# Cross-attention normalised in channel layout, with the denominators summed by VectorE

## Chip, cores and metric

One core of one Trainium2 chip. The metric is the device time of one launch in microseconds, and lower is better. The kernel before takes 371.97 us, the median of 3 runs (371.9 to 372.0).

## What is computed

A decoder layer over 16 sequences of 128 tokens with 256 channels: a retention block (8 heads of 32), a causal cross-attention with 16 heads of 16 channels, and a feed-forward block (256 to 1024 to 256, its own weights for each pair of sequences), each behind a layer norm and with a residual. The change touches only the cross-attention:

```python
scores = jnp.einsum('bhqd,bhkd->bhqk', qh, kh) * scale
scores = jnp.where(causal, -jnp.inf, scores)
attn = jax.nn.softmax(scores, axis=-1)
out = jnp.einsum('bhqk,bhkd->bhqd', attn, vh)
out = out.transpose(0, 2, 1, 3).reshape(b, s, DIM)
return out @ Wo + bo
```

## The kernel before

The work is cut into 8 steps of two sequences (NB = 2, T = 256 tokens). Three blocks run as a software pipeline: body(i) does retention of step a = i, cross-attention of step b = i - 1 and the feed-forward block of step c = i - 2. Bodies 0, 1 and 2 are written out, bodies 3 to 6 are a loop, and bodies 7 (no further retention input), 8 (no retention) and 9 (feed-forward only) are written out again. Each engine has its own body with a fixed order of instructions, and semaphores tie the engines together. All eight PSUM banks are in use and named: a0, a1, b0, b1k, b2k, b3, c0, c1; the trace leaves digits out, so it calls them a, b, b1k, b2k and c.

Attention of one step goes in eight units u, four per sequence (PR = 4), with four heads each (G = 4). For a unit, TensorE writes the scores; VectorE takes the maxima (negmax, L912); ScalarE takes the exponentials (prob, L596, four instructions); TensorE transposes the four 128x128 tiles into bank b1k (L1344); ScalarE copies the even units to probT (L558), VectorE the odd ones (L919); TensorE multiplies by v_pad, 32 columns a head: 16 values, a one, and zeros (`with_values`, L1347). So the sum of the probabilities comes out of the same matmul as channel 16 of each head. prob and probT have four buffers.

After four units (a sequence), ScalarE copies the products to pvT (`pv_out`, L639), TensorE turns them back into token layout with four transposes (`values_to_tokens`, L1366, instruction line L1371), VectorE takes the reciprocal of the sums (rden, L928) and multiplies (att, L930). After both sequences, TensorE transposes att again, into channel layout (`attention_transposes`, instruction line L1223), ScalarE copies it to attT_hi (L558), VectorE writes the remainder to attT_lo (L862), and TensorE multiplies by xWo (`attention_out`, L1379).

Around the change, in the order of each queue in a body of the loop:

- VectorE, from the last hidden split (L905) on: probT(1), varA (L1045, L1047), statistics of the next x (L842 to L849), maxima 4, probT(3), maxima 5, retT (L1109), maxima 6 and 7, xnA (L857), outT (L1127, two), probT(5), x (L1137, the retention's output with its residual), divide(0), probT(7), statistics of it, divide(1), cTB_lo (L862), xnB (L857), attT_lo (L862), x2b (L962), x (L956, the attention's output).
- TensorE, from the transposes of unit 5 on: a piece of the feed-forward product, values_to_tokens(0), the product of outT with W_sb, transposes of unit 6, values of units 4 and 5, transposes of xnA, transposes of unit 7, feed-forward, values of units 6 and 7, transposes of the context c_in, gate piece 0, values_to_tokens(1), gate pieces 1 and 2, attention_transposes, keys (cTB, xWk), attention_out.
- GpSimd takes the reciprocal square roots (rsA, rsB, rsC, rstA; L453), the low parts of the feed-forward weights (w_lo, L460 and L466), and sums with biases (L473, L480).

## Time and profile before

| | |
|---|---|
| median of 3 runs | 371.97 us |
| the profiled execution, whole | 369.38 us |
| its span, first to last instruction | 367.6 us |
| granted TensorE clock | 1.000 of full speed |
| TensorE matmul busy | 338.3 us, 92% |
| VectorE busy | 254.6 us, 69% |
| ScalarE busy | 238.9 us, 65% |
| GpSimd busy | 163.5 us, 44% |

Busy time says how long an engine had something in it, not whether it set the pace: matmuls overlap in the array, so a busy TensorE can still have been fed late. In a timeline, a row gives the start in us from the span's start, the busy time of the row, engine and line, what is written and read, and in brackets the idle time of the engine before the row with what ended it. Consecutive VectorE instructions overlap a little: of two 128x512 operations the second starts about 0.60 us after the first, though each is listed with 0.68 or 0.69 us.

### The profile page before, as it was taken

What the parts mean: (1) busy time and instruction counts of PE and PEld (TensorE: products, weight loads), DVE (VectorE), ACT (ScalarE), POOL (GpSimd) and SP (SyncE); (2) the same over time, 40 slices, a digit from 0 to 9 for tenths busy, and PEclk for the clock granted to TensorE, in tenths of its full rate; (3) what the DMA queues carried; (4) which work ended last, traced back from release to release, by engine and by line L of the source; (5) the groups of instructions that cost most, each with busy time, mean ns of one, the idle gap of its engine ahead of it and who ended that gap; (6) DMA issues with size and microseconds to landing.
All of it is one profiled execution on the core that took longest, in us unless ns stands there. A gap on an engine that the chain in (4) does not pass through costs nothing.

```text
span 367.6 us, 8998 instructions
## 1 busy us (share of the span) xinstructions
PE 338.3 (92%) x3283; PEld 280.1 (76%) x3299; DVE 254.6 (69%) x555; ACT 238.9 (65%) x586; POOL 163.5 (44%) x148
## 2 busy tenths in 40 slices
PE   7878679999999999999999999999999998989697
PEld 3657457987789877987789867987789866858596
DVE  5674786677766976677775976678765966482974
ACT  4552663776756866677847766677848764787551
POOL 4237150364615366363625457362634550445340
PEclk9999999999999999999999999999999999999999
DMA  5940102022031400413023400404014300013300
GB/s 151 307 172 1 31 2 107 37 62 85 1 112 78 144 0 17 171 33 110 0 66 120 143 0 14 169 7 137 0 47 141 116 6 10 30 16 116 116 29 30
DMA packets 22314, 26.97 MB, mean 73 GB/s; under 512 B 2896, under 2 KB 20112, under 8 KB 22288
## 3 DMA queue, kind: packets, MB, share of 16 engines
q1 hardware_dynamic: 21472, 26.52, 22.3%
q8 instruction: 17, 0.28, 0.3%
q10 hardware_dynamic: 816, 0.10, 0.2%
q14 instruction: 9, 0.07, 0.1%
HBM read 24.51 MB, written 2.10 MB: 72 GB/s over the span
## 4 chain that ended last, share of the span: by engine, by line
PE 77%; DVE 9%; issue 7%; ACT 4%; POOL 1%; DMA 1%; ACTq 0%; DVEq 0%; POOLq 0%
PE c L1208 22%; PE a L1208 16%; PE b L1208 14%; PE b1k L1344 7%; PE b1k L1208 6%; PE b2k L1208 4%; DVE negmax L912 2%; PE c L1371 2%; ACT prob L596 1%; ACT probT L558 1%; PE a L1223 1%; DVE scD L893 1%; PE b2k L1223 1%; DMA wk_c<-in_L_attn_Wk 1%; PE a L1301 1%
## 5 line engine op out<-in xcount | busy, mean ns | idle before, releaser
L460 POOL TENSOR_TENSOR w_lo<-w_in,w_hi 128x512 fp32r<-128x512 f32 x32 | 40.8, 1305 | 30.4 <-ACT w_hi L558 26.3
L596 ACT ACTIVATE prob<-b,negmax 128x128 f32<-128x128 f32 x124 | 36.1, 398 | 25.4 <-DVE negmax L912 25.4
L1344 PE MATMUL b1k<-ident,prob 128*128 128x128 f32 x256 | 40.0, 279 | 9.3 <-ACT probT L558 4.5
L466 POOL TENSOR_TENSOR w_lo<-w_in,w_hi 128x512 fp32r<-128x512 f32 x28 | 35.5, 1287 | 28.6 <-ACT w_hi L558 26.8
L453 POOL TENSOR_TENSOR rstA<-varA,minus_half 128x16 f32<-128x16 f32 x8 | 23.4, 2927 | 49.2 <-DVE varA L1047 49.2
L1344 PEld LDWEIGHTS b1k<-ident,prob 128*128 128x128 f32 x256 | 28.1, 140 | 17.3 <-ACT prob L596 7.2
L558 ACT ACTIVATE w_hi<-w_in 128x512 fp32r<-128x512 f32 x64 | 39.1, 653 | 2.6 <-PE b L1208 2.6
L1208 PE MATMUL c<-xTC_hi,w_hi 128*128 128x256 f32 x108 | 31.8, 294 | 0.8 <-DVE xTC_lo L862 0.8
L919 DVE COPY probT<-b1k 128x512 f32<-128x512 f32 x32 | 22.0, 687 | 13.1 <-PE b1k L1344 13.0
L1208 PE MATMUL c<-w_hi,h_hi 128*128 128x256 f32 x96 | 30.8, 321 | 0.1
L1208 PE MATMUL c<-xTC_lo,w_hi 128*128 128x256 f32 x108 | 30.5, 282 | 0.0
L1208 PE MATMUL c<-xTC_hi,w_lo 128*128 128x256 f32 x108 | 30.5, 282 | 0.0
L573 ACT ACTIVATE h_in<-c,b_cur 128x256 f32<-128x256 f32 x54 | 22.6, 472 | 11.4 <-PE c L1208 11.2
L912 DVE TENSOR_REDUCE negmax<-b 128x4 f32<-128x512 f32 x31 | 21.3, 687 | 12.5 <-PE b2k L1208 8.7
L1208 PE MATMUL c<-w_hi,h_lo 128*128 128x256 f32 x96 | 27.0, 281 | 0.0
L1208 PE MATMUL c<-w_lo,h_hi 128*128 128x256 f32 x96 | 26.9, 280 | 0.0
L453 POOL TENSOR_TENSOR rsC<-mvC,minus_half 128x2 f32<-128x2 f32 x8 | 5.7, 710 | 45.2 <-DVE mvC L849 45.2
L905 DVE TENSOR_TENSOR h_lo<-h_in,h_hi 128x512 fp32r<-128x512 f32 x32 | 24.5, 767 | 1.1
L558 ACT ACTIVATE probT<-b1k 128x512 f32<-128x512 f32 x32 | 20.8, 651 | 3.6 <-PE b1k L1344 3.6
L1208 PEld LDWEIGHTS c<-xTC_hi,w_hi 128*128 128x128 f32 x108 | 20.6, 190 | 2.7 <-issue 1.6
L1208 PEld LDWEIGHTS c<-w_hi,h_hi 128*128 128x128 f32 x96 | 18.0, 188 | 4.7 <-issue 3.2
L1208 PEld LDWEIGHTS c<-xTC_lo,w_hi 128*128 128x128 f32 x108 | 20.6, 191 | 0.0
(301 smaller groups left out, 1110.4 us busy)
## 6 DMA issues: line engine op xcount, KB each, us to landing
w_in<-in_L_ffn_w SPq DMA_DIRECT2D x16, 1024.0 KB, 5.6
x_in<-in_x SPq DMA_DIRECT2D x8, 256.0 KB, 2.8
c_in<-in_ctx SPq DMA_DIRECT2D x8, 256.0 KB, 2.9
out<-x2b SPq DMA_DIRECT2D x7, 256.0 KB, 2.2
b_cur<-in_L_ffn_b SPq DMA_DIRECT2D x8, 128.0 KB, 3.0
W_sb<-in_L_attn_W SPq DMA_DIRECT2D x2, 256.0 KB, 4.2
decay_sb<-in_decay SPq DMA_DIRECT2D x1, 512.0 KB, 3.8
h_in<-in_L_xattn_Wk SPq DMA_DIRECT2D x1, 256.0 KB, 4.3
```

The costliest lines, as they stand in the source:

```text
L453: pool.tensor_tensor(out, in_, minus_half[:, 0:n], ALU.pow).then_inc(s_out, 1)
L460: pool.tensor_tensor(w1_lo[:, :, part], w1_in[:, :, part], w1_hi[:, :, part].bitcast(F32), ALU.subtract).then_inc(s_w1lo, 1)
L466: pool.tensor_tensor(w2_lo[:, part, :], w2_in[:, part, :], w2_hi[:, part, :].bitcast(F32), ALU.subtract).then_inc(s_w2lo, 1)
L558: nc.scalar.activation(out, in_, ACT.Copy).then_inc(done, 1)
L573: ins = nc.scalar.activation(h_in[:, u, k, :], bank[:, k * T:(k + 1) * T], ACT.Gelu_apprx_tanh, bias=b1_cur[:, f:f + 1])
L596: ins = nc.scalar.activation(prob[:, u % PR, g, :], score_banks[u][:, g * P:(g + 1) * P], ACT.Exp, bias=negmax[:, u, g:g + 1], scale=-1.0)
L905: nc.vector.tensor_tensor(h_lo[:, part, :], h_in[:, u, :, :], h_hi[:, part, :].bitcast(F32), ALU.subtract).then_inc(s_hlo, 1)
L912: nc.vector.tensor_reduce(negmax[:, u, :], score_banks[u][:, :].rearrange("p (g m) -> p g m", g=G), AX_X, ALU.min).then_inc(s_max, 1)
L919: nc.vector.tensor_copy(probT[:, u % PR, :, :], b1k[:, :].rearrange("p (g n) -> p g n", g=G)).then_inc(s_pTd, 1)
L1208: return nc.tensor.matmul(out, lhsT, rhs, start=start, stop=stop)
L1223: ins = nc.tensor.transpose(out[:, col:col + P], src[:, b, k * P:(k + 1) * P], ident[:, :])
L1344: ins = nc.tensor.transpose(b1k[:, g * P:(g + 1) * P], prob[:, u % PR, g, :], ident[:, :])
```

## The change

Attention is normalised without going to token layout and back. v_pad no longer holds ones: a head's 16 values sit in the lower or the upper half of its 32 columns, depending on r, and the rest is zero. Two units with r = 2q and 2q + 1 accumulate into the same columns of one bank, so that the bank holds the unnormalised attention of both sequences already in channel layout (PV_BANK is c0 alone). The denominators come from `sums(u)`, one VectorE reduction of prob per unit, in all bodies but body 8; in body 8 they come from ScalarE's accumulator output of the exponentials. VectorE takes the reciprocals and copies them, each repeated 16 times, to rtok (`denominators(seq)`); TensorE transposes rtok into bank b3 (`reciprocals`, four transposes a step); ScalarE copies that to rdT; VectorE multiplies it with the bank (`normalise_attention`), ScalarE copies the result to attT_hi from SBUF, and VectorE writes attT_lo (`split_attention`). Removed are pvT, both copies to it, values_to_tokens, att and attention_transposes. The exponentials of unit u wait for sums(u - 4). xWo is loaded in the new channel order by 8 DMAs instead of 4, and GpSimd sets v_pad to zero with two 128x512 memsets instead of 128x32 and 128x480.

```diff
-WO_LOADS = 4
+WO_LOADS = 8
-        PV_BANK = [c0, b3]
+        PV_BANK = c0
@@ ScalarE @@
                     if u >= PR or later(b):
                         act.wait_ge(s_T, 8 * b + u - PR + 1)
+                    if do_a and (u >= PR or later(b)):
+                        act.wait_ge(s_den, 8 * b + u - PR + 1)
+                    if not do_a:
+                        act.wait_ge(s_den, 8 * b)
+                        if u % PR == 0:
+                            act.wait_ge(s_rden, 2 * b - 1 + u // PR)
                     for g in range(G):
                         ins = nc.scalar.activation(prob[:, u % PR, g, :], score_banks[u][:, g * P:(g + 1) * P],
-                                                   ACT.Exp, bias=negmax[:, u, g:g + 1], scale=-1.0)
+                                                   ACT.Exp, bias=negmax[:, u, g:g + 1], scale=-1.0,
+                                                   accum_out=None if do_a else den[:, u, g:g + 1])
-                    pv_out(1)
                     context(b1k)
-                    attention_out(b2k)
+                    reciprocals(b3)
+                    attention_out()
                     keys(b1k)
@@ VectorE @@
+                def sums(u):
+                    dve.wait_ge(s_prob, 8 * b + u + 1)
+                    nc.vector.tensor_reduce(den[:, u, :], prob[:, u % PR, :, :], AX_X, ALU.add).then_inc(s_den, 1)
+                    nc.vector.reciprocal(rden[:, seq, :], den[:, PR * seq:PR * (seq + 1), :]
+                                         .rearrange("p r g -> p (r g)")).then_inc(s_rden, 1)
                     dve.wait_ge(s_rden, 2 * b + seq + 1)
+                    of_head = rden[:, seq, :].rearrange("p (c r g) -> p c g r", c=C, r=2)
+                    nc.vector.tensor_copy(rtok[:, seq, :, :].rearrange("p c (g r e) -> p c g r e", g=G, r=2),
+                                          of_head.unsqueeze(4).broadcast_to([P, C, G, 2, XD])).then_inc(s_rexp, 1)
+                def normalise_attention():
+                    dve.wait_ge(s_pv, 8 * (b + 1))
+                    dve.wait_ge(s_rdT, b + 1)
+                    nc.vector.tensor_tensor(attT[:, :, :], pv_bank[:, :].rearrange("p (c t) -> p c t", c=C),
+                                            rdT[:, :, :], ALU.mult).then_inc(s_aT, 1)
...
                 if do_b:
+                    sums(0)
                     probT_odd(1)
+                    sums(1)
                 if do_a and do_b:
                     variances()
+                if do_b:
+                    sums(2)
                 if nextA and do_b:
                     next_x()
                 if do_b:
+                    sums(3)
                     maxima(4)
                     probT_odd(3)
                     maxima(5)
...
                 if do_b:
+                    sums(4)
                     maxima(6)
                     maxima(7)
+                    sums(5)
...
                 if do_b:
-                    divide(0)
+                    sums(6)
+                    denominators(0)
+                    sums(7)
                     probT_odd(7)
+                    denominators(1)
                 dve.wait_ge(s_x1, a + 1)
                 statistics(a, x1, statB, mvB, s_lnB)
                 if do_b:
-                    divide(1)
                     split_transposed(s_cTB, a, b1k, cTB_hi, cTB_lo, s_cTBlo)
+                    normalise_attention()
                 normalise(a, x1, mvB, rsB, xnB, s_rsB, s_xnB, s_TxB)
                 if do_b:
-                    split_transposed(s_attT, b, b2k, attT_hi, attT_lo, s_attTlo)
+                    split_attention()
@@ TensorE @@
-                    ins = mm(bank[VP * h:VP * (h + 1), r * P:(r + 1) * P], v_pad[:, bk, head, :],
-                             probT[:, u % PR, h, :])
+                    ins = mm(bank[VP * h:VP * (h + 1), col:col + P], v_pad[:, bk, head, :], probT[:, u % PR, h, :],
+                             start=(r % 2 == 0), stop=(r % 2 == 1))
-                if do_b:
-                    values_to_tokens(0)
...
                 if do_b and nextA:
                     context(b1k)
+                if do_b and nextA:
+                    reciprocals(b3)
                 if nextA:
                     gate(a + 1, 0)
-                if do_b and nextA:
-                    values_to_tokens(1)
-                if nextA:
                     gate(a + 1, 1)
                     gate(a + 1, 2)
                 if do_b and nextA:
-                    attention_transposes(b2k)
                     keys(b1k)
                     attention_out(b, b0)
```

In body 7 the same parts stand around the context and query input. In body 8, TensorE runs reciprocals(c0) and the values of units 6 and 7 ahead of up(2) and up(3), and both values_to_tokens and attention_transposes go; ScalarE leaves out both copies to pvT, and takes the second half of round_w2 between the first two GELUs instead of before them.

## Rows read from the trace of the kernel before

**Rows 1.** Part 4 of the page: the chain that ended last, shares by engine.

```profile
PE 77%; DVE 9%; issue 7%; ACT 4%; POOL 1%; DMA 1%; ACTq 0%; DVEq 0%; POOLq 0%
```

**Rows 2.** Timeline of VectorE in a body of the loop, hidden split to outT.

```profile
210.32 0.69 DVE L905 TENSOR_TENSOR h_lo<-h_in,h_hi 128x512 fp32r<-128x512 f32 x1
211.19 0.69 DVE L919 COPY probT<-b1k 128x512 f32<-128x512 f32 x1 [0.18 <-PE b1k L1344]
...
215.34 0.69 DVE L912 TENSOR_REDUCE negmax<-b 128x4 f32<-128x512 f32 x1 [1.24 <-PE b2k L1208]
216.66 0.69 DVE L919 COPY probT<-b1k 128x512 f32<-128x512 f32 x1 [0.63 <-PE b1k L1344]
...
220.30 0.87 DVE L1127 SCALAR_TENSOR_TENSOR outT<-a,gn_sb,silA 128x256 f32<-128x256 f32 x2
```

**Rows 3.** Timeline of TensorE: last piece before outT's product, and that product's start.

```profile
220.86 0.60 PE L1371 MATMUL c<-ident,pvT 128*128 128x128 f32 x4
221.30 0.63 PE L1208 MATMUL a<-W_sb,outT 128*128 128x256 f32 x2
```

**Rows 4.** VectorE in groups by line and form: busy, mean ns, idle before.

```profile
L912 DVE TENSOR_REDUCE negmax<-b 128x4 f32<-128x512 f32 x31 | 21.3, 687 | 12.5 <-PE b2k L1208 8.7 <-PE a L1208 2.7 <-PE c L1208 1.1
...
L1045 DVE TENSOR_REDUCE varA<-thA 128x16 f32<-128x512 f32 x8 | 5.5, 686 | 2.8 <-ACT thA L706 2.6
```

**Rows 5.** Timeline of VectorE, the tail of the same body.

```profile
223.26 0.69 DVE L1137 TENSOR_TENSOR x<-a,x_keep 128x512 f32<-128x512 f32 x1 [1.49 <-PE a L1208]
...
225.47 0.69 DVE L919 COPY probT<-b1k 128x512 f32<-128x512 f32 x1 [0.89 <-PE b1k L1344]
```

**Rows 6.** Timeline of TensorE, the tail of the same body.

```profile
226.64 0.66 PE L1223 MATMUL b1k<-ident,c_in 128*128 128x128 f32 x4
227.13 0.60 PE L1208 MATMUL a<-xTA,W_sb 128*128 128x256 f32 x2
227.57 0.60 PE L1371 MATMUL c<-ident,pvT 128*128 128x128 f32 x4
...
228.98 0.66 PE L1223 MATMUL b2k<-ident,att 128*128 128x128 f32 x4
229.57 0.39 PE L1208 MATMUL b1k<-cTB_hi,xWk_hi 128*128 128x256 f32 x1
...
231.10 0.34 PE L1208 MATMUL b<-xWo_hi,attT_hi 128*128 128x256 f32 x1
```

**Rows 7.** Timeline of TensorE in bodies 1 and 7: the start of outT's product.

```profile
54.48 1.78 PE L1208 MATMUL a<-W_sb,outT 128*128 128x256 f32 x7 [0.49 <-DVE outT L1127]
...
304.70 1.89 PE L1208 MATMUL a<-W_sb,outT 128*128 128x256 f32 x8
```

**Rows 8.** Timeline of VectorE in body 7: maxima 4, and outT.

```profile
298.67 0.69 DVE L912 TENSOR_REDUCE negmax<-b 128x4 f32<-128x512 f32 x1 [2.52 <-PE b2k L1208]
...
302.99 0.87 DVE L1127 SCALAR_TENSOR_TENSOR outT<-a,gn_sb,silA 128x256 f32<-128x256 f32 x2
```

**Rows 9.** Timeline of ScalarE in body 8: waits, then a one-column instruction.

```profile
325.64 1.14 ACT L596 ACTIVATE prob<-b2k,negmax 128x128 f32<-128x128 f32 x4 [0.49 <-DVE negmax L912]
...
328.86 0.60 ACT L558 ACTIVATE xTC_hi<-b 128x512 fp32r<-128x512 f32 x1 [0.21 <-PE b L1223]
...
333.80 0.20 ACT L680 ACTIVATE spare<-minus_half 128x1 f32<-128x1 f32 x1
333.91 1.14 ACT L558 ACTIVATE w_hi<-w_in 128x512 fp32r<-128x512 f32 x2
```

**Rows 10.** Hidden splits: durations, minimum/median/maximum; then VectorE and GpSimd at the maximum.

```profile
L902 DVE TENSOR_SCALAR h_hi<-h_in x32: 417/417/1529, 78.4 to 360.9; 128x512 fp32r<-128x512 f32 x32
...
342.81 1.53 DVE L902 TENSOR_SCALAR h_hi<-h_in 128x512 fp32r<-128x512 f32 x1
...
342.76 2.72 POOL L460 TENSOR_TENSOR w_lo<-w_in,w_hi 128x512 fp32r<-128x512 f32 x2 [3.16 <-ACT w_hi L558]
```

**Rows 11.** Timeline of GpSimd in the tail of the body: the sum with the bias.

```profile
225.62 1.28 POOL L480 TENSOR_TENSOR x2b<-x,b_cur 128x512 f32<-128x512 f32 x1
```

More of the change, by code:

```diff
@@ L148, in decoder_kernel @@
         probT = sb("probT", [P, PR, G, P])
-        pvT = sb("pvT", [P, 512])
+        den = sb("den", [P, 2 * PR, G])
         rden = sb("rden", [P, NB, XH])
-        att = sb("att", [P, NB, XH, XD])
+        rtok = sb("rtok", [P, NB, C, P])
+        rdT = sb("rdT", [P, C, T])
+        attT = sb("attT", [P, C, T])
         attT_hi = sb("attT_hi", [P, C, T], F32R)
@@ L445, in _ @@
                 .then_inc(s_const, 1)
-            pool.memset(v_pad[:, :, :, XD:XD + 1], 1.0).then_inc(s_const, 1)
-            pool.memset(v_pad[:, :, :, XD + 1:VP], 0.0).then_inc(s_const, 1)
+            for bk in range(NB):
+                pool.memset(v_pad[:, bk, :, :], 0.0).then_inc(s_const, 1)
             pool.wait_ge(s_const, 9)
@@ L562, in body @@
                 score_banks = banks_of(i)[1]
-                pv_banks = PV_BANK if do_a else PV_LAST
                 def gelu(u, bank):
@@ L637, in ffn_input, with reciprocals, attention_out @@
                     copy(xTC_hi[:, :, :], bank[:, :].rearrange("p (c t) -> p c t", c=C), s_xTC)
[L639 to L648 removed]
+                def reciprocals(bank):
+                    act.wait_ge(s_rT, b + 1)
+                    if later(b):
+                        act.wait_ge(s_aT, b)
+                    copy(rdT[:, :, :], bank[:, :].rearrange("p (c t) -> p c t", c=C), s_rdT)
+                def attention_out():
                     act.wait_ge(s_aT, b + 1)
[L650 removed]
+                    if later(b):
+                        act.wait_ge(s_yB, b)
+                    copy(attT_hi[:, :, :], attT[:, :, :], s_attT)
                 if do_c and not do_b:
@@ L934, in ffn_statistics, with split_attention @@
+                def split_attention():
+                    dve.wait_ge(s_attT, b + 1)
+                    nc.vector.tensor_tensor(attT_lo[:, :, :], attT[:, :, :], attT_hi[:, :, :].bitcast(F32),
+                                            ALU.subtract).then_inc(s_attTlo, 1)
                 def ffn_statistics():
@@ L1157, in body @@
                 if do_b:
-                    divide(1)
                     split_transposed(s_cTB, a, b1k, cTB_hi, cTB_lo, s_cTBlo)
+                    normalise_attention()
                 normalise(a, x1, mvB, rsB, xnB, s_rsB, s_xnB, s_TxB)
                 if do_b:
-                    split_transposed(s_attT, b, b2k, attT_hi, attT_lo, s_attTlo)
+                    split_attention()
                 if do_c:
```

130 lines of the change are left out of this document (55 added, 75 removed).

## Prediction

> **What bounds the kernel now.** I read the chain of work that ended last first: three quarters and more of the span is TensorE [rows 1], which runs at full granted clock. So the question is where TensorE waits or runs work that the change removes, and what feeds it late. Next I read the timeline of one body of the loop, engine by engine; a body is 41.80 us long, as the same rows return at that distance. Two places matter. The first is the product of outT with W_sb. TensorE comes to it straight from the transposes of pvT at 220.86, which take 0.44 us from start to start, and begins it at 221.30 [rows 3]. VectorE's outT starts at 220.30 and ends at 221.17 [rows 2]. The two arrive within 0.1 us of each other: anything that makes outT later makes TensorE later, and anything that makes TensorE earlier there gains nothing unless outT comes earlier too. The second place is the tail of the body, from x on VectorE (223.26 [rows 5]) to attention_out on TensorE (231.10 [rows 6]). There VectorE idles 0.89 us before probT(7) [rows 5].
>
> **The change part by part, for a body of the loop.**
>
> *Removed from TensorE.* Eight transposes net a body (two groups of four for pvT, one for att, against one for rtok). A group costs 0.44 us of TensorE's time [rows 3]; that of the second sequence starts at 227.57 [rows 6], so at most 2 x 0.44 = 0.88 us a body, if nothing else is late.
>
> *Added to VectorE: sums.* The nearest rows are the maxima, 687 ns for the same 128x512 input from PSUM, and varA, 686 ns for 512 columns from SBUF [rows 4]. Consecutive 512-column operations follow each other at 0.60 us (h_lo at 210.32 is listed with 0.69, and its follower could have started at 210.93, if 0.18 us of wait are taken off 211.19 and the handover [rows 2]). I take 0.60 us of VectorE's queue for each sum; the bounds are 0.54 (a tenth less, as nothing in the rows allows more) and 0.69 (no overlap at all).
>
> Six of the eight sums (0 to 5) stand ahead of outT in VectorE's queue: 6 x 0.60 = 3.6 us. What can absorb them is VectorE's idle time between the last hidden split and outT: 0.18 + 1.24 + 0.63 = 2.05 us [rows 2]. Walking it through: sums(0) starts at 210.93, probT(1) at 211.53 (0.34 late), so TensorE's transposes of unit 2 and the second half of the scores are about 0.3 late; maxima(4) starts at 216.08 instead of 215.34 because sums(1), (2) and (3) with varA and the statistics fill the queue; probT(3) waits for TensorE until 216.95, maxima(5) is 0.3 late, sums(4) starts at 218.75, maxima(6) at 219.35, sums(5) at 220.55, xnA at 221.15, outT at 221.79. It ends at 222.66 instead of 221.17. TensorE reaches that product at about 221.2 (transposes of unit 5 are 0.3 late, since the exponentials of unit 4 and probT(4) are, and 0.44 us of pvT transposes are gone) and then stands idle until 222.75. Cost: 222.75 - 221.30 = 1.45 us. The gain of the first removed group is swallowed whole.
>
> *The tail.* From the product on, TensorE and x are 1.45 late: x at 224.71. Behind it VectorE now has sums(6), reciprocal, copy, sums(7), and only then probT(7): 0.60 + 0.29 + 0.35 + 0.60 = 1.84 us after x's 0.60, so probT(7) starts at 227.15; before it started 2.21 us after x [rows 5], now 2.44. The 0.89 us of idle time hide most of it. TensorE's values of unit 7 follow at 227.9 and the context transposes at 228.2, against 226.64 [rows 6]. Then denominators(1) is ready at 228.45 and the transposes of rtok start at about 228.65 with no wait to speak of; six gate matmuls, 1.41 us (228.98 less 227.13, less one group of 0.44 [rows 6]), bring TensorE to the keys at 230.5, when cTB_lo has just ended at 230.4. That is 0.93 after the old 229.57: here two groups fewer show. The keys take 1.53 us (231.10 less 229.57), so TensorE is free at 232.0. But attT_lo now hangs on a longer chain: ScalarE's copy of rdT (to 230.0), normalise_attention behind cTB_lo (230.35 to 231.04), ScalarE's copy to attT_hi (to 231.7), split_attention (231.75 to 232.44), since xnB fits between. attention_out starts at 232.5: 1.40 us late against 231.10. So the tail gives back 0.05 us, and the second and third group are lost to a 0.5 us wait there. What follows (retention's queries, the attention's output, the feed-forward) comes in TensorE's order from there and shifts by the same 1.40. Cost of a body: **+1.40 us, five bodies (2 to 6): +7.0 us**. Bounds: with 0.54 a sum, 0.4 less; with 0.69, 0.5 more, so 1.0 to 1.9 a body.
>
> *Bodies 1 and 7.* In body 1 TensorE already waits 0.49 us for outT [rows 7], and VectorE has no idle time between the statistics and outT: sums 2 to 5 count in full and about 0.1 more from probT(1), so +2.5 us. In body 7 there is no next x to normalise; a wait of 2.52 us before maxima(4) takes sums 0 to 3 [rows 8], but for the 0.3 to 0.4 us by which probT(1) is late, and sums 4 and 5 push outT by 1.5 us in all, of which 0.84 is slack (it ended at 303.86, its product began at 304.70 [rows 7, 8]). The tail there adds sums 6 and 7 and two copies against one group of transposes: I make it +1.3 us. Together **+3.8 us**; bounds 2.5 to 5.
>
> *Body 8 and the end.* No sums there; 32 exponentials write an accumulator. The trace shows no such operation. From below it costs nothing; from above as much as a one-column ScalarE instruction listed at 0.20 us. That instruction held the queue for 0.11 us (333.80 to 333.91 [rows 9]), which I take, being the nearest in size: 32 x 0.11 = 3.5 us on ScalarE, which feeds TensorE here. Against that: one copy to pvT less before the last exponentials (0.5 us), ScalarE's waits of 0.49 to 0.21 us, three in all with 0.93 us [rows 9], and three groups less on TensorE (1.3 us). 3.5 - 0.5 - 0.9 - 1.3 = **+0.8 us**; bounds -2.5 (accumulators free) and +3.5.
>
> *Edits at nothing.* Four more DMA issues and larger memsets of v_pad come before the first attention; ScalarE's first weights wait for other work, and if that cover is gone it is at most 2 us. v_pad in two instructions instead of one is some 0.1 us more of VectorE, ahead of a wait of about 2 us for retention's scores. with_values keeps its matmuls. The copy to rtok has 256 columns and I take 0.35 us, less than h_hi's 0.42 for 512 [rows 10].
>
> Sum: 7.0 + 3.8 + 0.8 = 11.6 us. The profiled execution took 369.38 us with a span of 367.6, so I expect a span near 379.2 and an execution of 381.0; the median stands 2.6 above the profiled one: 371.97 + 11.6 = **383.6 us**.
>
> The Trainium skill, page "VectorE: DVE Perf Modes", section "The TRN2 errata", gives VectorE a fixed part of 58 cycles for SBUF sources and 120 for PSUM ones at 0.96 GHz, so a sum should be 0.065 us cheaper than a maximum. The trace doesn't agree: 686 ns from SBUF against 687 ns from PSUM [rows 4]. By the page, six sums ahead of outT would cost 0.4 us less a body, and the total would be about 381, an estimate; I go by the rows.
>
> **The rivals.** *(a) The sums hide, and the transposes saved count.* Then TensorE gains two groups in each of seven bodies, 7 x 0.88 = 6.2 us: about 366 us, faster. This decides only if VectorE's idle time before outT is above the sums' 3.6 us; it is 2.05 [rows 2]. For it speaks only that VectorE is busy for 69% of the span, an average over stages. Chance 0.05. *(b) Half hidden.* Sums are cheaper in the queue, or TensorE's slack in other places absorbs lateness, so that losses and gains nearly cancel: 371 to 376 us. Chance 0.08, half of it within 0.2%. *(c) VectorE and GpSimd get in each other's way.* One h_hi, beside GpSimd's w_lo, took 1529 ns where the median is 417 [rows 10]. The copy to rtok is of the same kind (SBUF to SBUF, one source). In the new order the first one starts at about 226.2 in a body, when GpSimd's sum with the bias (225.62 to 226.90 [rows 11]) may still run, and everything behind it on VectorE, probT(7) first, would wait: up to 1.1 us a body, 7 x 1.1 = 7.8 us, about 391 us. Against it: GpSimd's work may end before. Chance 0.17. The Trainium skill, page "GPSIMD Engine Reference", section "Specifications", says that GpSimd shares its SBUF interface with VectorE when that runs in a two-port mode or with two SBUF inputs; the one long h_hi agrees, and the sums, which have one SBUF input and no such mode, would be exempt.
>
> **How the numbers follow.** Forecast 0.70, at 378 to 388 by the bounds above (bodies 5 x 1.0 to 1.9, bodies 1 and 7 2.5 to 5, body 8 -2.5 to +3.5, not all at one end); (a) 0.05, (b) 0.08, (c) 0.17. The range, 376 to 391, leaves out (a), (b), what lies below 376, and the far end of (c). About 0.2% is what a measurement of this kernel can tell from no change. Faster: (a) and a quarter of (b), 0.07; same 0.04; slower 0.89.
>
> **What would show it.** Right: a body of 43.2 us; TensorE idle 1 to 1.6 us before outT's product, ended by VectorE; VectorE without idle time from the last hidden split to maxima(4); sums listed with 0.69 us and 0.60 us apart; attention_out waiting for attT_lo. Wrong: sums much shorter than the maxima; a body under 42 us; waits of VectorE before outT that I have not seen fill up; the copy to rtok at over 1 us, which is (c).

## The result, and the profile of the changed kernel

| | before | changed |
|---|---|---|
| median of the runs | 371.94 us | 393.61 us (392.45 to 394.64) |
| ratio, 95% interval | | 1.0608 (1.0571 to 1.0644) |
| profiled execution, its span | 369.38, 367.6 us | 393.7, 391.9 us |
| granted clock, mean | 1.000 | 0.974 |
| TensorE's share of the chain that ended last | 77% | 55% |

The change makes the kernel 21.7 us slower. The forecast was 11.6 us, the range ended at 391: right in sign, wrong in size. The profiled execution of the kernel before was granted the full clock; others of it that were measured beside the experiments were granted 0.991 to 1.000 and took 369.1 to 372.0 us. So the spans below, which differ by 24.3 us, set the changed kernel against a quick execution of the one before; the medians differ by 21.7. One of the four executions of e2 below, at 383.67 us, was in a slower state of the chip and is left out of its ratio. First the page of the changed kernel: busy shares, the clock line of the 40 slices, and the chain [rows 1].

```profile
PE 340.1 (87%) x3219; PEld 281.4 (72%) x3235; DVE 296.5 (76%) x627; ACT 239.3 (61%) x610; POOL 165.7 (42%) x148
...
PEclk9999989999699998999999999999999999899989
...
PE 55%; DVE 23%; issue 9%; ACT 8%; POOL 3%; DMA 1%; DVEq 0%; ACTq 0%; POOLq 0%
```

VectorE has 23% of the chain where it had 9%, and the clock, 9 in every slice before, has fallen in five places: in body 1, twice in the loop, and twice behind the last product of outT. Next the timeline of TensorE at the one place that the prediction rests on, the first piece of outT's product in each of the seven bodies that have it [rows 3, 7]: start, duration of the group, and in brackets the idle time before.

```profile
56.56 1.99 PE L1252 MATMUL a<-W_sb,outT 128*128 128x256 f32 x8 [0.70 <-DVE outT L1165]
...
100.70 3.78 PE L1252 MATMUL a<-W_sb,outT 128*128 128x256 f32 x8 [2.66 <-DVE outT L1165]
...
147.64 3.63 PE L1252 MATMUL a<-W_sb,outT 128*128 128x256 f32 x8 [2.72 <-DVE outT L1165]
...
193.58 1.99 PE L1252 MATMUL a<-W_sb,outT 128*128 128x256 f32 x8 [2.72 <-DVE outT L1165]
...
237.88 1.99 PE L1252 MATMUL a<-W_sb,outT 128*128 128x256 f32 x8 [2.72 <-DVE outT L1165]
...
282.18 1.99 PE L1252 MATMUL a<-W_sb,outT 128*128 128x256 f32 x8 [2.72 <-DVE outT L1165]
...
324.32 1.99 PE L1252 MATMUL a<-W_sb,outT 128*128 128x256 f32 x8 [0.67 <-DVE outT L1165]
```

An undisturbed body is 282.18 - 237.88 = 44.30 us, not the 43.2 of the forecast, and TensorE stands idle for 2.72 us before the product, not 1.0 to 1.6. Two products take 3.7 instead of 2.0 us: those ran at half clock, and the bodies behind them last 46.94 and 45.94 us. From the last of these products to the end it is 67.6 us, against 62.9 before (367.6 less 304.70 [rows 7]). The six distances between products were 41.42, four times 41.80, and 41.60 us before (its timeline has the second product at 95.90 and the sixth at 263.10). So the 24.3 us by which the span grew are: 2.1 ahead of the first product; 2.7, 5.1, 4.1, 2.5, 2.5 and 0.5 in the six distances, of which 2.6 and 1.6 in the second and third are the half clock's (46.94 and 45.94 less 44.30); and 4.7 behind the last product. The 2.1 and the 4.7 hold half clock too, as shown below.

What VectorE did ahead of the product at 237.88, and GpSimd beside it:

```profile
233.78 0.68 DVE L922 TENSOR_REDUCE negmax<-b2k 128x4 f32<-128x512 f32 x1
234.37 0.68 DVE L934 TENSOR_REDUCE den<-prob 128x4 f32<-128x512 f32 x1
234.97 2.07 DVE L863 TENSOR_SCALAR xnA<-x_in,mvA,rsA 128x256 f32<-128x256 f32 x2
236.96 0.86 DVE L1165 SCALAR_TENSOR_TENSOR outT<-a,gn_sb,silA 128x256 f32<-128x256 f32 x2
```

```profile
234.33 5.06 POOL L463 TENSOR_TENSOR w_lo<-w_in,w_hi 128x512 fp32r<-128x512 f32 x4 [2.00 <-ACT w_hi L561]
```

The sum holds the queue for 0.60 us (234.37 to 234.97) as forecast. But xnA, the normalised next x, takes 2.07 us for its two halves, where it took 0.73 before:

```profile
219.66 0.73 DVE L857 TENSOR_SCALAR xnA<-x_in,mvA,rsA 128x256 f32<-128x256 f32 x2
```

```profile
220.69 4.97 POOL L460 TENSOR_TENSOR w_lo<-w_in,w_hi 128x512 fp32r<-128x512 f32 x4 [2.96 <-ACT w_hi L558]
```

In the kernel before (these last two rows) xnA was 0.3 us ahead of GpSimd's w_lo: it ended at 220.39. The sums push xnA back, w_lo comes when ScalarE's w_hi is there, and now xnA starts 0.64 us into it.

### The profile page after: what moved, and what is told of

It is laid out like the page before. It is cut to its first block, busy times and chain, and to the rows that moved or that the text cites. A ratio compares the mean times of both kernels' runs of the same rounds, so it can differ in the third digit from the quotient of the medians.

```text
span 391.9 us, 8988 instructions
## 1 busy us (share of the span) xinstructions
PE 340.1 (87%) x3219; PEld 281.4 (72%) x3235; DVE 296.5 (76%) x627; ACT 239.3 (61%) x610; POOL 165.7 (42%) x148
## 4 chain that ended last, share of the span: by engine, by line
PE 55%; DVE 23%; issue 9%; ACT 8%; POOL 3%; DMA 1%; DVEq 0%; ACTq 0%; POOLq 0%
PE c L1252 16%; PE a L1252 12%; PE b L1252 11%; DVE negmax L922 6%; PE b1k L1386 4%; PE b2k L1252 3%; PE b1k L1252 3%; DVE xnA L863 3%; ACT prob L604 3%; DVE den L934 2%; DVE probT L929 2%; PE a L1267 1%; DVE outT L1165 1%; POOL w_lo L469 1%; ACT attT_hi L561 1%
## 5 line engine op out<-in xcount | busy, mean ns | idle before, releaser
L1386 PE MATMUL b1k<-ident,prob 128*128 128x128 f32 x256 | 41.0, 284 | 12.9 <-ACT prob L604 4.6
L463 POOL TENSOR_TENSOR w_lo<-w_in,w_hi 128x512 fp32r<-128x512 f32 x32 | 41.2, 1316 | 25.3 <-ACT w_hi L561 20.5
L469 POOL TENSOR_TENSOR w_lo<-w_in,w_hi 128x512 fp32r<-128x512 f32 x28 | 36.7, 1329 | 33.5 <-ACT w_hi L561 31.6
L1386 PEld LDWEIGHTS b1k<-ident,prob 128*128 128x128 f32 x256 | 29.4, 144 | 20.7 <-ACT prob L604 11.4
L934 DVE TENSOR_REDUCE den<-prob 128x4 f32<-128x512 f32 x56 | 37.9, 679 | 0.0
L561 ACT ACTIVATE probT<-b1k 128x512 f32<-128x512 f32 x32 | 19.8, 619 | 23.9 <-PE b1k L1386 23.6
L1252 PE MATMUL a<-W_sb,outT 128*128 128x256 f32 x64 | 19.4, 455 | 15.2 <-DVE outT L1165 15.2
L1252 PEld LDWEIGHTS a<-W_sb,outT 128*128 128x128 f32 x64 | 13.7, 225 | 19.2 <-DVE outT L1165 17.2
L456 POOL TENSOR_TENSOR rsB<-mvB,minus_half 128x2 f32<-128x2 f32 x8 | 5.6, 705 | 49.4 <-DVE mvB L855 49.4
L915 DVE TENSOR_TENSOR h_lo<-h_in,h_hi 128x512 fp32r<-128x512 f32 x32 | 25.4, 795 | 1.1
```

Source lines behind the costliest of these rows:

```text
L456: pool.tensor_tensor(out, in_, minus_half[:, 0:n], ALU.pow).then_inc(s_out, 1)
L463: pool.tensor_tensor(w1_lo[:, :, part], w1_in[:, :, part], w1_hi[:, :, part].bitcast(F32), ALU.subtract).then_inc(s_w1lo, 1)
L469: pool.tensor_tensor(w2_lo[:, part, :], w2_in[:, part, :], w2_hi[:, part, :].bitcast(F32), ALU.subtract).then_inc(s_w2lo, 1)
L561: nc.scalar.activation(out, in_, ACT.Copy).then_inc(done, 1)
L915: nc.vector.tensor_tensor(h_lo[:, part, :], h_in[:, u, :, :], h_hi[:, part, :].bitcast(F32), ALU.subtract).then_inc(s_hlo, 1)
L934: nc.vector.tensor_reduce(den[:, u, :], prob[:, u % PR, :, :], AX_X, ALU.add).then_inc(s_den, 1)
```

## The experiments

Each ratio is against the kernel before, measured beside it on the same chip, where its median was 370.3 to 371.7 us. That median moves with its own granted clock (370.3 us at 0.995, 371.7 us at 0.991), so two ratios can differ by up to 0.4% for that reason alone. Differences in per cent are of the time before. The changed kernel's ratio is 1.0608. "Body" is the distance of two products of outT in the loop.

### The collision at xnA: held off, and in the kernel before

e1 makes GpSimd wait for xnA before it starts w_lo, e11 does the same in the kernel before with sums added, and e4 adds only the sums to it.

```diff
                 if do_b and nextA and later(b):
+                    pool.wait_ge(s_xnA, 2 * (a + 2))
                     for u in range(UP):
                         w1_low(b, u)
```

> The changed kernel with one wait more: GpSimd starts the four low parts of the first weights (w_lo) only when VectorE has written the next xnA. Nothing is left out. Theory 1 (collision): in the changed kernel the two xnA instructions together take 2.07 us instead of 0.73, because GpSimd's w_lo now runs beside them; without it xnA is back at 0.73, outT's product starts 1.4 us earlier relative to the body in bodies 2 to 6, that is 7 us, and TensorE's fall to half clock after that wait (two bodies, about 4 us) becomes rarer: 382 to 388 us in all. Rival (sums alone): the queue is full anyway, the collision only moves to the next VectorE instructions with two SBUF inputs or a copy, or w_lo comes late for its readers: 392 to 395 us, as changed.

Measured: 386.35 us, ratio 1.0433 (1.0386 to 1.0480), as theory 1 had it, and 0.0175 below the changed kernel's ratio, whose interval it doesn't touch. The body is 43.6 us. VectorE and TensorE there:

```profile
229.88 0.73 DVE L864 TENSOR_SCALAR xnA<-x_in,mvA,rsA 128x256 f32<-128x256 f32 x2
230.52 0.87 DVE L1166 SCALAR_TENSOR_TENSOR outT<-a,gn_sb,silA 128x256 f32<-128x256 f32 x2
```

```profile
231.45 1.99 PE L1253 MATMUL a<-W_sb,outT 128*128 128x256 f32 x8 [1.38 <-DVE outT L1166]
237.14 0.42 PE L1253 MATMUL c<-probT,v_pad 128*32 128x128 f32 x8 [0.59 <-DVE probT L930]
241.55 0.39 PE L1253 MATMUL b<-xWo_hi,attT_hi 128*128 128x256 f32 x1 [0.27 <-DVE attT_lo L962]
```

With xnA at its old 0.73 us TensorE waits 1.38 us: the walk through VectorE's queue in the prediction gave 222.75 - 221.2 = 1.5. The collision, and the half clock that its longer waits bring, is some 6.5 us of the 22.6 (0.0175 of 372 us against 0.0608).

> The kernel before, with the 56 sums of the change added at the same places of VectorE's queue (bodies 1 to 7) and the exponentials' waits for them; their result is used by nothing, the output is complete. Nothing is left out. Theory 1 (the sums make outT late, directly and through the collision with GpSimd): outT is as late as in the changed kernel, 2.9 us a body, and the tail keeps its old length, so 390 to 396 us. Rival (the new normalisation, not the sums, costs the time): 372 to 380 us.

Measured: 396.51 us, 1.0702 (1.0663 to 1.0740). All the loss, and more, comes with the sums alone. At full clock its body is 45.3 us, one more than the changed kernel's: here both halves of xnA stand behind w_lo in most bodies, with 2.55 us together. xnA collides in more than half of its instructions (the tile's durations in ns, minimum, median and maximum):

```profile
L863 DVE TENSOR_SCALAR xnA<-x_in,mvA,rsA x16: 405/1277/1353, 6.2 to 284.3; 128x256 f32<-128x256 f32 x16
```

> The kernel before with the eight sums (results unused, it still normalises by the column of ones) and with GpSimd's w_lo held until xnA is done. Theory (the loss of sums alone is queue time of VectorE plus the collision at xnA and the half clock behind it): xnA at 404 ns everywhere, body about 43.3 to 44.0 instead of 45.3 to 46.6, 384 to 390 us in all, against 396.5 without the wait. Rival (the collision is a symptom of lateness and costs nothing by itself): 394 to 397 us.

Measured: 384.52 us, 1.0402 (1.0359 to 1.0445), 3.0% less than e4 for one wait; a body of 43.43 us, TensorE waiting 0.94 us for outT. So the collision is a cost of its own. With it held off, the body of e11 (old normalisation, sums added) is within 0.2 us of that of e1 (new normalisation): there the rest of the change (transposes, place of the normalisation) hardly counts either way.

### What the sums cost without their size

e2 sums 16 of the 128 columns of each head (under a third of the listed time: 0.21 us for 0.68; the denominators are then no denominators), e5 adds the wait of e1.

```diff
-nc.vector.tensor_reduce(den[:, u, :], prob[:, u % PR, :, :], AX_X, ALU.add)
+nc.vector.tensor_reduce(den[:, u, :], prob[:, u % PR, :, 0:16], AX_X, ALU.add)
```

> The changed kernel, but each sum reads 16 of the 128 columns of a head (64 instead of 512 in all), so the denominators leave out the rest of the probabilities; every instruction and wait stays. Theory 1: a sum drops from 0.60 to about 0.2 us of VectorE's queue, so outT comes about 2.4 us earlier; xnA then starts before GpSimd's w_lo and is back at 0.73 us; the body falls to 41.5 to 42 us and the whole to 372 to 378 us. Rival (the waits and the longer chain at the tail, not the sums' time, make it slow): 385 us or more. If the transposes that were saved count once VectorE is not late, 368 to 372.

Measured: 376.80 us, 1.0161 (1.0117 to 1.0205), inside theory 1's time, but not by its way: the body is 42.6 us and TensorE still waits 1.4 us for outT. The sum is listed with 210 ns, yet xnA still collides in the loop:

```profile
L934 DVE TENSOR_REDUCE den<-prob x56: 204/210/222, 44.1 to 314.9; 128x4 f32<-128x64 f32 x56
...
L863 DVE TENSOR_SCALAR xnA<-x_in,mvA,rsA x16: 403/408/1410, 6.2 to 266.5; 128x256 f32<-128x256 f32 x16
```

> Sums over 16 of 128 columns (the rest of the probabilities is left out of the denominators) together with GpSimd's wait for xnA. Theory: what kept the body at 42.6 us with short sums was the collision alone (xnA 1.73 us, and the first copy to rtok 1.09 instead of 0.29). The wait takes the first away, so outT is 1.0 us earlier and the body falls to 41.4 to 41.8 us: 369 to 373 us. But w_lo then runs later, 5 us long, and the copy to rtok may still meet it; if the collision merely moves there, the body stays at 42.3 to 42.6 and the whole at 375 to 377 us.

Measured: 372.90 us, 1.0059 (1.0028 to 1.0091); body 41.9 to 42.0 us. Cheap sums and no collision give nearly the body of before, 41.80, and not one shorter by the 0.88 us of transposes saved on TensorE. The sums aren't fully hidden even here: TensorE waits 0.44 us for outT, about one group of transposes. Rival (a) is settled by the changed kernel itself, where it waits 2.72 us; e17 below adds that without any wait for outT the body is still 41.9 us. What the transposes would bring with no sums at all, no run shows.

### Half clock

e7 keeps the changed kernel and gives TensorE eight bf16 matmuls (results unused) in its wait for outT.

```diff
+                    if do_b and nextA:
+                        for _ in range(8):
+                            mm(a1[:, :], awake[:, 0:P], awake[:, :])
                     pe.wait_ge(s_outT, 2 * (a + 1))
```

> The changed kernel with eight bf16 matmuls of 512 columns (about 1.7 us) on TensorE ahead of its wait for outT in bodies 1 to 6, written to bank a1, which the product then overwrites; nothing is left out. They fill most of a wait of 2.7 us. Theory (the idle wait lets the granted clock fall, and the half clock behind it costs about 2 us each time): the clock stays at its full level in these bodies and the run is 3 to 5 us faster than the changed kernel, 388 to 391 us, with less spread. Rival (the falls have another cause, or the fillers delay the product): 393 us or more.

Measured: 390.29 us, 1.0535 (1.0502 to 1.0569), 0.7% or 2.7 us less; every body of the loop is 44.3 us. The windows of the changed kernel (busy time and count of PE, PEld, DVE, ACT, POOL, then the granted clock, DMA share and GB/s), and below them the same stretch in e7:

```profile
98.00:100.00 2.00, 0.04 (x1) 0.00 (x0) 2.00 (x3) 2.00 (x9) 2.00 (x3) 0.95 0.00 0
100.00:102.00 2.00, 1.30 (x3) 1.12 (x4) 1.24 (x3) 0.69 (x2) 2.00 (x2) 0.50 0.00 0
```

```profile
100.00:102.00 2.00, 1.50 (x7) 0.49 (x5) 2.00 (x4) 2.00 (x8) 2.00 (x3) 1.00 0.00 0
102.00:104.00 2.00, 1.57 (x7) 1.41 (x8) 0.97 (x2) 0.42 (x1) 2.00 (x3) 1.00 0.00 0
```

TensorE idled for 2.66 us and came back at 0.50 of the clock, the 1.2 GHz level; with work in the gap it stayed at 1.00, the 2.4 GHz level. The same wait of 2.72 us left three later products at their full-clock 1.99 us, so a fall doesn't follow each such wait; one costs 1.6 to 2.6 us here. Nor does it need so long a one: in e13 a product behind a wait of 1.37 us ran at half clock.

```profile
231.42 3.68 PE L1253 MATMUL a<-W_sb,outT 128*128 128x256 f32 x8 [1.37 <-DVE outT L1166]
```

The other three falls of the changed kernel lie outside e7's bodies of the loop. In body 1 (first row; the second is e15, at full clock behind the same wait) it is 4.43 us from these transposes to the product at 56.56, against 3.24 in e15, so this fall is some 1.2 us of the 2.1 ahead of the first product.

```profile
52.13 1.12 PE L1386 MATMUL b1k<-ident,prob 128*128 128x128 f32 x4 [2.62 <-ACT prob L604]
```

```profile
52.49 0.66 PE L1387 MATMUL b1k<-ident,prob 128*128 128x128 f32 x4 [2.62 <-ACT prob L605]
```

Behind the last product there are two, by the windows of the changed kernel (0.69 and 0.61 of the clock):

```profile
330.00:335.00 5.00, 3.47 (x23) 3.28 (x24) 4.25 (x9) 1.19 (x2) 0.00 (x0) 0.69 0.16 52
...
372.00:376.00 4.00, 3.22 (x16) 3.23 (x17) 3.38 (x6) 0.60 (x1) 3.20 (x3) 0.61 0.20 68
```

### The sums in other places

e6 has the wait, and sums 4 and 5 moved from ahead of xnA to behind probT(5). e8 has the wait, sums also in body 8, sums placed where VectorE waited, and outT ahead of xnA.

```diff
                 if do_b:
-                    sums(4)
                     maxima(6)
                     maxima(7)
-                    sums(5)
...
                     probT_odd(5)
+                    sums(4)
+                    sums(5)
```

> The changed kernel with GpSimd's wait for xnA and with sums(4) and sums(5) moved from before outT to behind probT(5), where VectorE idles 1.49 us for TensorE; nothing is left out. Theory (what is ahead of outT in VectorE's queue counts in full): outT comes 1.2 us earlier than with the wait alone, so the body goes from 43.6 to 42.4 us, and the whole from 386 to 378 to 380 us. Rival (the total of VectorE's work, not its place, sets the body): 384 us or more.

Measured: 378.18 us, 1.0224 (1.0160 to 1.0287), body 42.4 us, the theory's figures. Two sums off the path to outT are worth 1.2 us a body: what a sum costs depends on its side of outT.

> All that the runs so far point to, nothing left out: GpSimd's wait for xnA, VectorE's sums in body 8 too in place of the accumulators, sums(1), (2) and (3) each in a gap of VectorE's queue, sums(4) to (6) behind probT(5), and outT ahead of xnA. Theory: outT then starts within 0.1 us of its old place, TensorE reaches its product 0.4 us earlier than before, the tail gives 0.1 to 0.2 us: a body of 41.3 to 41.7 us and 368 to 374 us in all, about the kernel before. Rival (VectorE's total work keeps the tail late): a body of 42.3 us or more, 376 us or more.

Measured: 379.62 us, 1.0258 (1.0221 to 1.0295), body 42.75 us: the rival's figures, not the theory's. TensorE no longer waits for outT, but with xnA later GpSimd's w_lo is later too (227.19 to 232.2), its sum x2b follows at 232.19, and the collision lands where rival (c) had put it, on the copies to rtok:

```profile
230.20 0.90 DVE L941 COPY rtok<-rden 128x256 f32<-128x256 f32 x1
...
232.48 1.13 DVE L941 COPY rtok<-rden 128x256 f32<-128x256 f32 x1
```

### The end

e3 uses sums in body 8 too; e9 lets ScalarE round W2 ahead of that body's GELUs, so that GpSimd gets w2_lo earlier; e13 is e9 with the wait of e1.

```diff
                     round_w2(0)
+                    round_w2(1)
                     probT_even(6)
+                    round_w2(2)
+                    round_w2(3)
                     reciprocals(c0)
...
                     gelu(0, UP_BEFORE_LAST[0])
-                    round_w2(1)
                     gelu(1, UP_BEFORE_LAST[1])
-                    round_w2(2)
-                    round_w2(3)
```

> The changed kernel with VectorE's sums in body 8 too, and no accumulators: exponentials as before the change. Nothing is left out. Theory 1: reading the accumulator takes ScalarE about 0.095 us of queue for each of 32 exponentials, 3 us, and body 8 with the end got 2.6 us longer than before; VectorE has gaps there for eight sums (4.8 us), so body 8 gets 1 to 3 us shorter: 390.5 to 392.5 us. Rival (body 8 is set by the order of TensorE's queue or by GpSimd's late w_lo): within 1 us of the changed kernel, or slower.

Measured: 392.60 us, 1.0595 (1.0555 to 1.0634); 67.1 us behind the last product. Sums or accumulators in body 8: no difference within the intervals. That alone doesn't clear the accumulators, since both could cost the same; e14 below does.

> The changed kernel, but in body 8 ScalarE rounds the three remaining blocks of W2 ahead of that body's GELUs, so that GpSimd gets its subtractions for w2_lo earlier and its queue is free when it has to compute rsC. Theory (the end is late because GpSimd computes rsC behind w2_lo, about 1.6 us late, and because its subtractions lie beside VectorE's h_hi and h_lo): rsC begins within 0.3 us of mvC, from the last product of outT to the end 65 to 66.3 us instead of 67.6, about 391.5 to 392.5 us in all. Rival (rsC was late but not what the end hangs on; ScalarE's rounding ahead of the GELUs costs as much): 67 to 69 us for that stretch, 393 to 395 us in all. Bodies 1 to 7 as in the changed kernel, 44.3 us each in the loop, by both.

Measured: 393.34 us, 1.0626 (1.0590 to 1.0661), no faster by the median; the profiled execution was the fastest of five, 389.04 us, with 64.4 us behind the last product. GpSimd in the changed kernel, and in e9:

```profile
368.10 2.74 POOL L463 TENSOR_TENSOR w_lo<-w_in,w_hi 128x512 fp32r<-128x512 f32 x2
370.80 1.15 POOL L456 TENSOR_TENSOR rsC<-mvC,minus_half 128x2 f32<-128x2 f32 x1
```

```profile
367.78 0.81 POOL L456 TENSOR_TENSOR rsC<-mvC,minus_half 128x2 f32<-128x2 f32 x1 [2.21 <-DVE mvC L855]
```

In the changed kernel rsC stands behind w_lo without idle time and TensorE waits 4.06 us for xnC; in e9 it starts when mvC is there and TensorE waits 2.46 (in the kernel before 2.00). The fall of the clock behind xnC is gone in e9 too. The mechanism was shown, its worth not, with half clock coming and going.

> The changed kernel with GpSimd's w_lo held until xnA is done, and body 8's rounding of W2 ahead of its GELUs. Against the wait alone (386.35 us, last product of outT to the end 66.0 us): theory (GpSimd's rsC behind w2_lo makes the end late) 63.0 to 64.5 us for that stretch, 383 to 385 us in all. Rival (the end hangs on something else; the shorter end seen before was a matter of the clock): 65.5 us or more, 386 to 387 us.

Measured: 385.13 us, 1.0370 (1.0324 to 1.0415), 0.63% or 2.3 us below e1 by the ratios, but 1.2 us by the medians, and the intervals still touch; 64.6 us behind the last product against 66.0 in e1, with one fall of the clock in each. So GpSimd's order of work is worth 1.2 to 2.3 us directly: TensorE's wait for xnC is 1.6 us shorter. What is left of the 4.7 us is half clock, by e14: it has e13's two edits and sums 4 and 5 moved, no fall behind the last product, and takes 62.75 us from there to the end, no more than the 62.9 before, with the accumulators in it.

### Accumulators instead of sums

e10 takes the denominators from ScalarE's accumulators in every body.

```diff
-accum_out=None if do_a else den[:, u, g:g + 1])
+accum_out=den[:, u, g:g + 1])
...
-                    sums(0)
```

> The changed kernel with the denominators from ScalarE's accumulators in every body and no sums on VectorE. Theory (the sums are what makes the change slow, and an accumulator holds ScalarE for about 0.1 us): VectorE is again within 0.3 us of TensorE at outT's product, ScalarE has 32 x 0.1 = 3.2 us more a body and each unit of four exponentials takes about 1.4 instead of 1.0 us; where TensorE transposes units 3 to 5 it waits some 0.3 to 0.6 us; a body of 42.0 to 42.8 us, 374 to 380 us in all, 13 to 20 us less than the changed kernel. Rival (ScalarE becomes the bound: every exponential stands in the chain): a body of 44 us or more, 387 us or more. Against both: if xnA is still beside GpSimd's w_lo it will be listed with over 1 us in part of the bodies, which adds up to 0.6 us a body; the first blocks of w_hi come later from a busier ScalarE, so I expect a median of xnA near 0.41.

Measured: 383.70 us, 1.0359 (1.0316 to 1.0402), body 43.6 us: between theory and rival, and outside the theory's 42.8. Waits for outT are gone, but TensorE waits at the transposes of the probabilities and the scores:

```profile
217.81 0.66 PE L1372 MATMUL b1k<-ident,prob 128*128 128x128 f32 x4 [0.53 <-ACT probT L561]
219.43 0.63 PE L1372 MATMUL b1k<-ident,prob 128*128 128x128 f32 x4 [0.25 <-DVE probT L929]
221.33 0.38 PE L1238 MATMUL a<-mask_bf,ident_bf 128*128 128x512 bf16 x1 [0.69 <-ACT prob L604]
```

With some 2.9 us of such waits in a body, accumulators everywhere cost about what the sums cost without the collision (e1: 43.6 us, and 0.7% slower, with intervals that touch). xnA doesn't collide here (413 ns at most). As the change stands, its sums in the loop are the worse choice, 2.5% slower than e10; with GpSimd's wait the two are hardly apart, and with sums 4 and 5 moved (e6) the sums are the better one.

### Towards a version without loss

> All that the runs so far speak for, together: w_lo held until xnA is done, sums 4 and 5 behind probT(5), W2's rounding of body 8 ahead of the GELUs, and the copy to rtok on ScalarE (eight instructions a body, four for each sequence, one of them ahead of the copies of the context, about 0.2 us each). Theory (VectorE's queue before probT(7) and attT_lo sets the tail; 0.29 us leave it twice): a body of 41.9 to 42.3 us against 42.4, about 373 to 376 us in all. Rival (ScalarE's 1.6 us more stand in the tail ahead of rdT and attT_hi, which TensorE waits for): a body of 42.6 to 43.4 us, 378 to 384 us. Neither expects it under the kernel before.

Measured: 382.02 us, 1.0321 (1.0280 to 1.0362), body 43.0 us: the rival. TensorE waits 1.26 us for ScalarE's last rtok. That kernel without the move of the copies is e14, and e15 adds five bf16 matmuls for TensorE in body 1's wait.

> The same with sums 4 and 5 behind probT(5), the copies to rtok on VectorE. Against the late sums without the W2 edit (378.18 us, body 42.4): theory 375 to 376.5 us. Against the run with the copies to rtok on ScalarE (382.02 us, body 43.0): if the move of the copies cost 0.6 us a body, 377 us or less here with a body of 42.4; if the W2 edit is what cost there, 380 us or more.

Measured: 376.73 us, 1.0155 (1.0113 to 1.0196), body 42.45 us. The move of the copies cost 1.7% by the ratios, 5.3 us by the medians.

> The same as the run before in this call, with five more bf16 matmuls of 512 columns (into a bank that is free, results unused) on TensorE in body 1, in its wait of 1.4 us ahead of the transposes of unit 1. Theory (the half clock at 42 to 46 us makes body 1 some 1.2 to 1.5 us longer in every kernel with the change): granted clock 1.0 there and the first product of outT in the loop at 55.5 to 56.0 instead of 57.2, 1.0 to 1.5 us less in all. Rival (body 1 waits for VectorE or ScalarE anyway): full clock, but the product at the same time and no gain.

Measured: 373.92 us, 1.0073 (1.0051 to 1.0095), first product at 55.73 instead of 57.12 us, as its theory says, and 2.8 us less by the medians than e14, more than the theory's 1.0 to 1.5. The clock lines of the pages of e14 and e15:

```profile
PEclk9999889999999999999999999999999999999999
```

```profile
PEclk9999999999999999999999999999999999999989
```

e16 keeps e15 and orders sums(7) ahead of the first copy, and in body 7 probT(7) ahead of sums and copies, keys ahead of rtok's transposes. e17 adds rnA ahead of probT(3), and eight matmuls for TensorE ahead of the last feed-forward.

```diff
                     sums(6)
-                    denominators(0)
                     sums(7)
+                    denominators(0)
                     probT_odd(7)
```

> The kernel of e15 with three orders changed: in the loop sums(7) ahead of the first copy to rtok, so that this copy starts when GpSimd's w_lo is nearly over; in body 7 probT(7) ahead of sums 6 and 7 and of both copies, and keys ahead of the transposes of rtok. Theory (the copy, listed with 0.95 us, and probT(7) behind it are what the loop still loses): copy below 0.5 us, TensorE's wait for probT(7) 0.1 to 0.2 instead of 0.60 us, a body of 41.9 to 42.1 us instead of 42.4, body 7 one to two us shorter; 369.5 to 371.5 us in all against 373.9. Rival (the tail hangs on attT_lo, so what is won at probT(7) is waited for there): body 42.3 to 42.4 us, 373 us or more.

Measured: 373.45 us, 1.0069 (1.0039 to 1.0098). In the loop the theory holds: body 42.0 us, the first copy down from 0.95 us (e15) to 0.38 (e16), no wait for probT(7):

```profile
228.13 0.95 DVE L949 COPY rtok<-rden 128x256 f32<-128x256 f32 x1
```

```profile
227.62 0.38 DVE L949 COPY rtok<-rden 128x256 f32<-128x256 f32 x1
```

But what the loop won is given back outside it: the clock line is at 8 in one slice of body 1, and it is 65.2 us from the last product to the end where e15 had 64.0, with two slices at 8 there for e15's one. In body 7 TensorE's wait of 2.11 us for probT(7) has become waits of 0.81 and 1.51 us for xnB and cTB_lo, and the added fall starts at the second. Whether it would be there without the new order stays open.

> The kernel of e16 with rnA (retT's source) computed ahead of probT(3) on VectorE, where it waits 0.29 us, and with eight bf16 matmuls of 512 columns (results unused) for TensorE in its wait of 2.5 us ahead of the last feed-forward, behind which half clock was seen. Theory: outT 0.2 to 0.35 us earlier, TensorE's wait for it gone, body 0.2 us shorter; the clock 1.0 to the end, up to 1.2 us; together 1 to 2.5 us less than e16. Rival (probT(3) 0.25 us later costs what outT gains; and the end was at full clock without help): within 0.5 us of e16.

Measured: 373.38 us, 1.0074 (1.0044 to 1.0104), within 0.5 us of e16, the rival. TensorE's wait for outT is gone (body 41.9 us) and the clock holds at the last feed-forward, but it still falls in bodies 1 and 7. No version with the change beats the kernel before; the best are 0.7% behind it.

## Why the prediction was wrong

*Bound and place: right.* TensorE and VectorE meet at outT's product, and all that VectorE gets ahead of outT counts there; e6 shows it from the other side.

*The price of a sum: right.* 0.60 us of queue, 0.68 listed. The bound below, 0.54, did not come to bear. The table of the Trainium skill, page "VectorE: DVE Perf Modes", section "The TRN2 errata", would make a sum from SBUF 0.065 us cheaper than a maximum from PSUM. The trace of the changed kernel doesn't show that: the sums have a mean of 679 ns, the maxima of 681 to 685.

*The walk through a body: right but for one operation.* Without the collision (e1) the wait at outT is 1.38 us against 1.5, and the body 43.6 against 43.2. The 0.4 us are in the tail, where the wait of e1 moved w_lo under the copy to rtok (0.93 us at 234.96) and TensorE waits 0.59 us for probT(7); in the changed kernel itself the copy took its 0.29 us, less than the 0.35 assumed, and attention_out waited 0.28 us for attT_lo as described, for 0.5 us forecast.

*The step that failed: xnA at no extra cost.* The walk put "xnA at 221.15" and outT 0.64 us behind it, and did not hold that time against GpSimd's row. w_lo starts at 220.69 in the kernel before; whatever pushes xnA by more than 0.3 us pushes it under w_lo. It was put at nothing without a look at that row, and cost 2.07 - 0.73 = 1.34 us ahead of outT, and made the body 44.30 - 43.2 = 1.1 us longer than the walk's, 5.5 in five. Rival (c) had the mechanism and the price (up to 1.1 us a body, 391 us), and the chance 0.17, but looked for it at the new instruction, the copy to rtok, where it did not happen [rows 11]. The example it went by was h_hi beside w_lo [rows 10], a TENSOR_SCALAR as xnA is, and xnA was a step of the walk.

The Trainium skill, page "VectorE: DVE Perf Modes", section "Mode 2×_2P — use both read ports for one tensor", says that a tensor_scalar or a copy of fp32 data in SBUF uses both of VectorE's read ports. The traces agree with that as the mark of what collides: xnA, h_hi and the copy to rtok grow beside GpSimd's subtractions, the sums never (674 to 686 ns over 56). It is not the only mark: h_lo, a subtraction with two inputs in SBUF, grows as well (0.69 to 1.67 us).

*The clock: not foreseen.* A forecast with TensorE idle 1.5 us at one place had no term for half clock. The clock was put at nothing, and it fell five times. That cost 4.3 us in the loop of the profiled execution (2.7 us by e7's ratio, 3.3 by its median), some 1.2 us in body 1, and a part of the end. The kernel before isn't free of it in each execution either (0.991 to 1.000).

*Bodies 1 and 7: 3.8 us forecast.* Ahead of the first product it is 2.1 us for 2.5, but 1.2 of them are half clock, so the nearness is luck and the sums cost some 0.9 us there. Body 7 can't be told apart from body 8 in one number, but TensorE's wait for probT(7) there was 2.11 us where before had 1.24.

*Body 8: the accumulator priced rightly, the end missed.* An accumulator holds ScalarE for about 0.1 us, near the 0.11 taken:

```profile
342.15 0.37 ACT L604 ACTIVATE prob<-b,negmax 128x128 f32<-128x128 f32 x1 [0.89 <-DVE negmax L922]
342.41 0.19 ACT L604 ACTIVATION_READ_ACCUMULATOR prob<-b,negmax 128x1 f32 x1
342.51 0.36 ACT L604 ACTIVATE prob<-b,negmax 128x128 f32<-128x128 f32 x1
```

From one exponential to the next it is 0.36 us with it, where four without one follow each other at 0.26 (three steps in 1.14 less the last one's 0.37 [rows 9]). But the end grew by 4.7 us, not 0.8, with sums as with accumulators: GpSimd's w2_lo, triggered by ScalarE's later rounding, stood ahead of rsC, and the clock fell twice. The later rounding is an edit of the change itself; the prediction had no term for it and no row for GpSimd's queue there.

*The sum.* In the profiled executions the five distances of the loop grew by 17.0 us for 7.0 forecast: 4.3 us more are half clock, and of the other 5.7 the collision at xnA is 5.5. The rest of the span grew by 7.3 us for 4.6 forecast (3.8 and 0.8): the 2.7 us more are rsC's place (1.2 to 2.3) and three more falls of the clock, against which the sums' own cost there was less than forecast. 11.6 + 5.7 + 4.3 + 2.7 = 24.3 us. The medians differ by only 21.7, with a kernel before that was itself not always at full clock. And e13, which has neither the collision at xnA nor rsC behind w_lo, is 3.7% or 13.8 us slower than before (13.4 by the medians): near the forecast, with some half clock left in it (0.982), so that agreement is in part luck too.

## What to carry to other kernels

Where an edit makes an engine late, list every operation that moves with it and hold its new time against the other engines' rows, not only the new instructions: an old instruction that ran just ahead of a GpSimd stretch can take three times as long inside it. A wait that brings such a pair apart cost GpSimd nothing in e1, where it had been idle for 3.5 us, but it moved w_lo beside the copy to rtok, for 0.4 us a body: look at once for the next operation that the moved work now lies beside. Where TensorE's waits grow, a fall of its clock belongs among the costs.

## What the runs showed of the hardware

VectorE's xnA (two halves, 256 columns each) takes 407 ns alone and up to 1410 (e2) beside GpSimd's 128x512 subtraction; a copy of 256 columns 293 and up to 1130 (e8). The subtraction of h_lo with two SBUF inputs grows from 0.69 to 1.67 us. Reductions, and outT with one input in PSUM, are untouched. GpSimd's own times hardly move (4.97 to 5.06 us for four). An ACTIVATE with an accumulator adds an instruction listed with 0.19 to 0.36 us that holds the queue for about 0.1. TensorE came back at half clock behind two of five waits of 2.7 us in the loop, behind one of 2.6 us in body 1 and, in e13, behind one of 1.4 us, and at full clock behind others just as long.
